# Eight unread products behind the first transposes of the maxima in both self attentions of a two-lane decoder, and the order of the two lanes written anew

## Chip, cores and metric

The kernel runs on one core of a Trainium2 chip, as one program. The metric is the device time of one execution in microseconds, the median of several runs. TensorE (PE) does the matrix products and the transposes, VectorE (DVE), ScalarE (ACT) and GpSimd (POOL) do the rest, and SyncE (SP) issues the DMAs. A profile comes from one more execution.

## What is computed

A pre-norm decoder of two layers runs over x of shape (4, 256, 128), with a context of the same shape. Each layer is a self attention, a cross attention and a feed-forward part, and each is added to x:

```python
x = x + _L0_attn_ref(_layernorm(x), Wq, Wk, Wv, rel_bias_table, ln_gamma, ln_beta)
x = x + _L0_xattn_ref(_layernorm(x), ctx, ctx, Wq, Wk, Wv, Wo, bo, mask)
x = x + _L0_ffn_ref(_layernorm(x), w1, conv_w, conv_b, w2)       # quantized, with a convolution
x = x + _L1_attn_ref(_layernorm(x), Wq, Wk, Wv, Wp, bp)          # causal, alibi, grouped keys
x = x + _L1_xattn_ref(_layernorm(x), ctx, ctx, ...)
x = x + _L1_ffn_ref(_layernorm(x), ...)                          # eight experts and a shared one
# the softmax of the first self attention, 16 heads of width 8:
attn = softmax(einsum('bhqd,bhkd->bhqk', q, k) * scale)
attn = attn + rel_bias_table[i - j + 255]
```

## The kernel before

The four batches are split over two lanes, A (batches 0 and 1) and B (batches 2 and 3). A lane is a full copy of the six stages with its own SBUF half and its own four PSUM banks, `bank[0]` to `bank[3]`; in the rows the names begin with `A_` or `B_`, and `l0a` and `l1a` are the two self attentions, `l0x` and `l1x` the cross attentions, `ffn` and `moe` the feed-forward parts. A third short program W (`weight_levels`) quantizes weights at the start, and L loads late weights.

Every engine works through one queue in program order. How the lanes share it is written out by hand in the table `TURNS`: for each engine a string such as `A4 W1 A7`, by which `merged` lets lane A emit four pieces, W one piece, A seven, and so on. A piece is what a lane's program emits between two `yield`s. So whatever stands first in an engine's queue and waits holds up what is behind it, the other lane's work too.

Both self attentions use the class `Attention`. It computes the scores twice:

- with queries on the partitions (`tensor_S` L226 and `tensor_S_pair` L296 in layer 0, L231 and L234 in layer 1), from which VectorE takes each row's maximum, negated (`vector_max`, L324), into `nmax`;
- with keys on the partitions (`tensor_E_pair` L310, or `tensor_E` L262, L263 and L266), whose exponentials ScalarE takes (`scalar_exp`, L358) for the products with the values (`tensor_PV`, L286).

For the second pass the maxima must stand in extra rows of the queries. `vector_parts` splits the maxima of a batch into three bf16 parts (L339 to L348), `tensor_shift` transposes them on TensorE into `bank[0]` (L242), `vector_shiftT` copies them to SBUF (L352), and `sync_shift` writes them into the queries by DMA (L252). The first `tensor_E` of a batch waits for that DMA. This is done once per lane, layer and batch of the lane (b = 0 and b = 1). For b = 1 the maxima are made during the second pass of b = 0.

Other rows that the text names: L662 transposes the stacks of split queries and keys, L647 projects x, L706 transposes finished outputs; L1247 and L1254 are the transposes and the last product of the quantized feed-forward part; L1616 transposes outputs in layer 1; L1816 is a product of a bf16 tile `same_token` with `other_token` (128x512) in the last cross attention. `bank[2]` is one of the two banks that the second pass writes into; between the transposes and the first E nothing in it is needed.

Of the kernel before, what the change touches and what calls it, by code (L numbers as in the profile page):

```python
# [175 lines left out]
class Attention:  # L176
# [59 lines left out]
        ins.then_inc(self.s_s.sem, 1)  # L236

    def tensor_shift(self, pe, b):
        pe.wait_ge(*self.s_parts(b + 1))
        view = self.bank[0][:, 0:P].bitcast(BF16)  # L240
        for c in range(SB):
            ins = pe.transpose(view[:, c * P:(c + 1) * P], self.parts[:, b, c, :], self.w["ident_bf"][:])  # L242
        ins.then_inc(self.s_tp.sem, 1)

    def sync_shift(self, sp, b):

        sp.wait_ge(*self.s_shT(b + 1))
        rows = P // self.G
        for j in range(self.G):
            dst = self.queries(b)[rows * j + self.row:rows * j + self.row + 3]  # L250
            src = self.shiftT[32 * j:32 * j + 3 * self.columns, b, :]
            sp.dma_start(dst, src).then_inc(self.s_q.sem, 16)  # L252
# [2117 lines left out]
def course(lane, name, eng):  # L2370

    for st in lane.plan:
# [9 lines left out]

TURNS = {
    "tensor":
# [8 lines left out]
    "vector":  # L2393
# [9 lines left out]
    "scalar":  # L2403
# [5 lines left out]
    "gpsimd":  # L2409
        "A12 B1 A3 B2 A1 B13 A11 B1 A1 B1 A1 B2 A1 B1 A2 B1 A1 B1 A1 B1 A2 B1 A1 B2 A2 B1 A1 B6 A1 B2 A1 B1 A3 B2 A1 B1 A1 B7 A8 B2 A2 B2 A1 B2 A2 B2 A1 B3 A1 "  # L2410
        "B1 A1 B2 A7 B1 A4 B3 A1 B1 A1 B9 A1 B1 A1 B2",
    "sync":
        "W3 A1 W10 B1 A2 B2 L1 A6 L1 A3 B5 A1 B5 A2 B2 A1 B1",
}


# [153 lines left out]
```

## Time and profile before

| | |
|---|---|
| time, median of 3 runs | 623.69 us (620.76 to 624.16) |
| the profiled execution, its own time | 619.47 us |
| its span, first to last instruction | 617.5 us |
| mean granted TensorE clock | 0.954 |
| busy share | PE 86%, PE weight loads 53%, DVE 69%, ACT 52%, POOL 31% |

The clock is given as a share of full speed: 1.0 is 2.4 GHz, 0.5 is 1.2 GHz. In a timeline row the numbers are the start and the length in us of a run of equal instructions, and the bracket at the end says how long the engine was idle before it and what ended that.

### The profile page before, as it was taken

The page shows a single profiled execution, that of the slowest core. Times are in us where ns is not written, and L with a number is a line of the kernel's source. Part 1 is how long each engine was busy: PE and PEld are TensorE (multiplying, and loading weights), DVE is VectorE, ACT ScalarE, POOL GpSimd, SP SyncE. Part 2 cuts the span into 40 slices and gives each one's busy share as a digit, 9 for nine tenths or more (in the row PEclk, how much of TensorE's full clock was granted, in tenths as well). Part 3 has the DMA queues.
Part 4 walks back from the last instruction along what each step waited for, and adds up shares of the span by engine and source line. Part 5 has one row for each costly group of instructions (what it writes and reads, how often), then busy time and mean ns, then how long its engine had stood idle before and what let it go on. Part 6 is the DMA issues. An engine that isn't in the chain of part 4 may idle for free. (4 is left out here: it accounts for less than half of the span.)

```text
span 617.5 us, 12861 instructions
## 1 busy us (share of the span) xinstructions
PE 529.0 (86%) x4880; PEld 327.9 (53%) x4890; DVE 424.6 (69%) x1037; ACT 323.5 (52%) x807; POOL 192.1 (31%) x288
## 2 busy tenths in 40 slices
PE   2668787999999999778986489978988999999894
PEld 1433343344555656446554355766666867655453
DVE  6885764654463654798779876847557577889994
ACT  1423445567576674695733536554666555362440
POOL 3743200043245443432620031001113122435653
PEclk9965999999999999989997889999999999999998
DMA  8700000000030000000256005300000000303001
GB/s 299 267 1 2 2 2 3 1 3 2 1 136 3 1 1 1 2 2 1 80 143 243 3 17 156 97 11 3 4 2 2 3 3 1 138 2 137 2 1 34
DMA packets 25815, 27.92 MB, mean 45 GB/s; under 512 B 18177, under 2 KB 22794, under 8 KB 24858
## 3 DMA queue, kind: packets, MB, share of 16 engines
q1 hardware_dynamic: 25754, 27.10, 13.1%
q8 instruction: 39, 0.64, 0.4%
q14 instruction: 22, 0.18, 0.1%
HBM read 22.14 MB, written 4.75 MB: 44 GB/s over the span
## 5 line engine op out<-in xcount | busy, mean ns | idle before, releaser
L811 POOL TENSOR_TENSOR A_l0x_prob<-A_l0x_prob,A_l0x_inverted_sums 128x256 f32<-128x256 f32 (+1 forms) x32 | 25.9, 829 | 56.6 <-DVE A_l0x_inverted_sums L922 56.6
L811 POOL TENSOR_TENSOR B_l0x_prob<-B_l0x_prob,B_l0x_inverted_sums 128x256 f32<-128x256 f32 (+1 forms) x32 | 26.5, 848 | 45.1 <-DVE B_l0x_inverted_sums L922 45.1
L2080 PE MATMUL B_banks<-B_moe_xT,w_moe_rows 128*128 128x512 f32 x72 | 33.8, 596 | 1.7 <-DVE B_moe_h L2047 1.7
L2080 PE MATMUL A_banks<-A_moe_xT,w_moe_rows 128*128 128x512 f32 x72 | 34.3, 597 | 0.0
L324 DVE TENSOR_REDUCE B_l0a_nmax<-B_banks 128x2 f32<-128x512 f32 x32 | 21.4, 688 | 15.2 <-PE B_banks L226 11.9
L905 DVE TENSOR_REDUCE A_l0x_nmax<-A_banks 128x2 f32<-128x256 f32 (+1 forms) x32 | 16.3, 552 | 22.6 <-PE A_banks L980 22.5
L358 ACT ACTIVATE A_l0a_expT<-A_banks 128x512 f32<-128x512 f32 x32 | 18.3, 599 | 22.0 <-PE A_banks L310 22.0
L829 ACT ACTIVATE B_l0x_prob<-B_banks,B_l0x_nmax 128x128 f32<-128x128 f32 x64 | 26.0, 420 | 5.9 <-DVE B_l0x_nmax L905 5.7
L324 DVE TENSOR_REDUCE A_l0a_nmax<-A_banks 128x2 f32<-128x512 f32 x32 | 21.3, 688 | 9.8 <-PE A_banks L226 8.0
L829 ACT ACTIVATE A_l0x_prob<-A_banks,A_l0x_nmax 128x128 f32<-128x128 f32 x64 | 26.1, 425 | 1.7 <-DVE A_l0x_nmax L905 1.7
L846 ACT ACTIVATE A_l0x_probT<-A_banks 128x384 f32<-128x384 f32 x32 | 15.8, 493 | 19.3 <-PE A_banks L992 19.1
L846 ACT ACTIVATE B_l0x_probT<-B_banks 128x384 f32<-128x384 f32 x32 | 15.7, 490 | 15.9 <-PE B_banks L992 15.8
L324 DVE TENSOR_REDUCE B_l1a_nmax<-B_banks 128x2 f32<-128x512 f32 (+1 forms) x24 | 16.2, 689 | 9.9 <-PE B_banks L234 9.7
L358 ACT ACTIVATE B_l0a_expT<-B_banks 128x512 f32<-128x512 f32 x32 | 18.6, 601 | 8.2 <-PE B_banks L310 8.1
L358 ACT ACTIVATE A_l1a_expT<-A_banks 128x384 f32<-128x384 f32 x32 | 15.3, 494 | 14.5 <-PE A_banks L266 14.5
L358 ACT ACTIVATE B_l1a_expT<-B_banks 128x384 f32<-128x384 f32 x32 | 15.5, 491 | 14.0 <-PE B_banks L266 13.9
L1976 ACT ACTIVATE B_moe_h<-B_banks,w_moe_rest_rows 128x512 f32<-128x512 f32 x18 | 12.3, 686 | 19.7 <-PE B_banks L2080 19.6
L2080 PEld LDWEIGHTS B_banks<-B_moe_xT,w_moe_rows 128*128 128x128 f32 x72 | 12.8, 190 | 14.7 <-issue 12.0
L905 DVE TENSOR_REDUCE B_l0x_nmax<-B_banks 128x2 f32<-128x256 f32 (+1 forms) x32 | 16.2, 548 | 5.9 <-PE B_banks L980 5.9
L1709 POOL TENSOR_TENSOR A_l1x_prob<-A_l1x_prob,A_l1x_rz 128x512 f32<-128x512 f32 x8 | 8.3, 1042 | 38.2 <-DVE A_l1x_rz L1790 38.2
L1976 ACT ACTIVATE A_moe_h<-A_banks,w_moe_rest_rows 128x512 f32<-128x512 f32 x18 | 12.1, 680 | 13.8 <-PE A_banks L2080 13.7
L992 PE MATMUL B_banks<-w_const_rows,B_l0x_prob 128*128 128x128 f32 x96 | 16.6, 283 | 3.0 <-POOL B_l0x_prob L811 1.4
(609 smaller groups left out, 1570.7 us busy)
## 6 DMA issues: line engine op xcount, KB each, us to landing
w_toeplitz_rows<-in_toeplitz_rows SPq DMA_DIRECT2D x1, 3072.0 KB, 15.3
w_moe_rows<-in_moe_rows SPq DMA_DIRECT2D x1, 2304.0 KB, 9.6
w_l1x_rows<-in_l1x_rows SPq DMA_DIRECT2D x1, 2048.0 KB, 7.8
A_l1x_values<-A_l1a_v_tokens SPq DMA_DIRECT2D x4, 512.0 KB, 3.5
A_l1x_v_groups<-A_l1x_values SPq DMA_DIRECT2D x16, 128.0 KB, 3.1
B_l1x_values<-B_l1a_v_tokens SPq DMA_DIRECT2D x4, 512.0 KB, 3.5
B_l1x_v_groups<-B_l1x_values SPq DMA_DIRECT2D x16, 128.0 KB, 3.1
w_l0x_vo_rows<-in_l0x_vo_rows SPq DMA_DIRECT2D x1, 1024.0 KB, 9.0
```

The lines of the kernel that those rows point to most:

```text
L324: dve.tensor_reduce(out, scores, AX, ALU.max, negate=True).then_inc(self.s_mx.sem, 1)
L358: act.activation(self.expT[:, u % self.ring, :], self.exp_bank(u)[:, 0:self.W], ACT.Exp, scale=self.scale).then_inc(self.s_p.sem, 1)
L811: ins = pool.tensor_tensor(pair, pair, bcast(rz[:, g % 2, i, :], 2, n), ALU.mult)
L829: ins = act.activation(prob[:, u % RING, at:at + n], bank[u % 2][:, at:at + n], ACT.Exp, bias=nmax[:, b, i, h:h + 1], accum_out=zsum[:, g ...
L846: act.activation(probT[:, u % 4, :], bank[2][:, 0:W], ACT.Copy).then_inc(s_pt.sem, 1)
L905: ins = dve.tensor_reduce(nmax[:, b, i, 2 * c:2 * c + 2], lane.banks[:, 0:2, at:at + n], AX, ALU.max, negate=True)
L992: ins = pe.transpose(bank[2][:, c * P:(c + 1) * P], prob[:, u % RING, c * P:(c + 1) * P], w["ident"][:])
L1709: pool.tensor_tensor(pr, pr, bcast(rz[:, n % 2, :], BL, 64), ALU.mult).then_inc(s_pn.sem, 1)
L1976: act.activation(h1[:, n % 2, :], hidden_bank(2 * n)[:, :], ACT.Identity, bias=w["moe_b1"][:, e, part:part + 1]).then_inc(s_h1.sem, 1)
L2080: pe.matmul(hidden_bank(k)[:, :], w["moe_w3" if which else "moe_w1"][:, ORDER[i], part, :], xT[:], start=True, stop=True).then_inc(s_h.sem, 1)
```

## The change

Two things are edited. In `tensor_shift`, for b = 0 alone, eight matrix products of the bf16 identity with the 128x512 tile `other_token` follow the two transposes. They write `bank[2]`, each with `start=True`, and nobody reads it. They wait for nothing of their own and signal nothing. That is four times in the program: lanes A and B, layers 0 and 1, so 32 products. And all five strings of `TURNS` are written anew.

```diff
     def tensor_shift(self, pe, b):
         pe.wait_ge(*self.s_parts(b + 1))
         view = self.bank[0][:, 0:P].bitcast(BF16)
         for c in range(SB):
             ins = pe.transpose(view[:, c * P:(c + 1) * P], self.parts[:, b, c, :], self.w["ident_bf"][:])
         ins.then_inc(self.s_tp.sem, 1)
+        if b == 0:
+            for _ in range(8):
+                pe.matmul(self.bank[2][:, :], self.w["ident_bf"][:], self.w["other_token"][:].rearrange("p i k -> p (i k)"), start=True,
+                          stop=True, skip_group_check=True)
...
 TURNS = {
     "tensor":
-        "A4 W1 A7 W1 A20 B1 A4 B1 A1 B1 A3 B1 A3 B1 A3 B1 A1 B1 A1 B1 A3 B1 A2 B2 A3 B1 A2 B2 A5 B2 A2 B1 A3 B1 A2 B2 A5 B3 A2 B3 A3 B1 A3 B1 A1 B4 A4 B1 A2 B2 "
+        "A4 W1 A6 W1 A23 B2 A2 B1 A2 B1 A6 B1 A4 B1 A2 B2 A2 B1 A5 B2 A2 B1 A3 B1 A1 B1 A1 B1 A3 B1 A1 B1 A1 B3 A6 B3 A2 B3 A2 B3 A4 B3 A2 B1 A1 B1 A1 B1 A2 B1 "
...
     "sync":
-        "W3 A1 W10 B1 A2 B2 L1 A6 L1 A3 B5 A1 B5 A2 B2 A1 B1",
+        "W2 A1 W11 B1 A2 B2 L1 A6 L1 A3 B5 A1 B5 A2 B2 A1 B1",
```

In the changed kernel all lines behind the new ones are six higher: L310 is L316, L286 is L292, L1247 is L1253. The order of TensorE's instructions at lane A's first maxima, layer 0, before:

```order
L172 MATMUL B_banks<-w_const_rows,B_l0a_xn 128x128 x4
L296 MATMUL A_banks<-A_l0a_qkT 128x256 x4
L647 MATMUL B_banks<-w_l0a_rows,B_l0a_xT 128x384
L662 MATMUL A_banks<-w_ident_bf,A_l0a_expT 128x128 x4
L242 MATMUL A_banks<-w_ident_bf,A_l0a_parts 128x128 x2
L647 MATMUL B_banks<-w_l0a_rows,B_l0a_xT 128x384
L310 MATMUL A_banks<-A_l0a_qkT 128x256 x4
L226 MATMUL A_banks<-A_l0a_qkT 128x256 x2
```

The same place in the changed kernel:

```order
L653 MATMUL B_banks<-w_l0a_rows,B_l0a_xT 128x384
L302 MATMUL A_banks<-A_l0a_qkT 128x256 x4
L653 MATMUL B_banks<-w_l0a_rows,B_l0a_xT 128x384
L668 MATMUL A_banks<-w_ident_bf,A_l0a_expT 128x128 x4
L244 MATMUL A_banks<-w_ident_bf,A_l0a_parts 128x128 x2
L248 MATMUL A_banks<-w_other_token,w_ident_bf 128x512 x8
L316 MATMUL A_banks<-A_l0a_qkT 128x256 x4
L226 MATMUL A_banks<-A_l0a_qkT 128x256 x4
```

B's second projection, which stood between the transposes and the first E, now stands before the transposes, and the eight products are what is left between them.

TensorE at lane A's first maxima in layer 1, while lane B is at the end of its quantized feed-forward part, before:

```order
L242 MATMUL A_banks<-w_ident_bf,A_l1a_parts 128x128 x2
L1247 MATMUL B_banks<-w_ident_bf,B_ffn_q_228 128x128 x4
L262 MATMUL A_banks<-A_l1a_qT,A_l1a_kT 128x256
L263 MATMUL A_banks<-A_l1a_qT,A_l1a_kT 128x128
L266 MATMUL A_banks<-w_mask_k,w_ident_bf 128x128 x2
L231 MATMUL A_banks<-A_l1a_kT,A_l1a_qT 128x256 x2
```

And in the changed kernel:

```order
L244 MATMUL A_banks<-w_ident_bf,A_l1a_parts 128x128 x2
L248 MATMUL A_banks<-w_other_token,w_ident_bf 128x512 x8
L1253 MATMUL B_banks<-w_ident_bf,B_ffn_q_228 128x128 x16
L1260 MATMUL B_banks<-w_ffn_q,B_ffn_q2T 128x128 x16
L268 MATMUL A_banks<-A_l1a_qT,A_l1a_kT 128x256
L269 MATMUL A_banks<-A_l1a_qT,A_l1a_kT 128x128
```

The first E of lane A now stands behind all 16 transposes and all 16 products of lane B's feed-forward part; before, four transposes stood ahead of it.

TensorE at lane B's first maxima in layer 0, in the changed kernel; before, the same rows stood there without L248:

```order
L316 MATMUL A_banks<-A_l0a_qkT 128x256 x4
L244 MATMUL B_banks<-w_ident_bf,B_l0a_parts 128x128 x2
L248 MATMUL B_banks<-w_other_token,w_ident_bf 128x512 x8
L712 MATMUL A_banks<-w_const_rows,A_l0a_xT 128x128 x2
L316 MATMUL A_banks<-A_l0a_qkT 128x256 x4
```

Here work of lane A follows the products at once.

## Rows read from the trace of the kernel before

**Rows 1.** The page: span, TensorE's busy share and its granted clock in 40 slices.

```profile
span 617.5 us, 12861 instructions
...
PE   2668787999999999778986489978988999999894
...
PEclk9965999999999999989997889999999999999998
```

**Rows 2.** Busy time by window (columns PE, PEld, DVE, ACT, POOL, then the clock).

```profile
42.00:48.80 6.80, 2.77 (x22) 1.32 (x21) 3.61 (x11) 3.13 (x9) 4.09 (x11) 1.00 0.01 4
48.80:62.50 13.70, 12.73 (x81) 5.28 (x80) 7.16 (x14) 4.16 (x11) 2.68 (x8) 0.50 0.00 1
...
349.20:356.00 6.80, 3.70 (x28) 3.07 (x29) 3.73 (x9) 3.80 (x6) 0.00 (x0) 0.50 0.02 6
...
120.00:240.00 120.00, 118.00 (x895) 64.61 (x888) 62.54 (x181) 80.56 (x265) 47.33 (x63) 1.00 0.05 19
```

**Rows 3.** Timeline at lane A's first maxima, layer 0.

```profile
43.43 0.27 PE L242 MATMUL A_banks<-w_ident_bf,A_l0a_parts 128*128 128x128 bf16 x2 [0.73 <-ACT A_l0a_qkT L511]
...
43.54 0.86 PE L647 MATMUL B_banks<-w_l0a_rows,B_l0a_xT 128*128 128x384 f32 x2
43.74 0.29 DVE L352 COPY A_l0a_shiftT<-A_banks 128x256 bf16<-128x256 bf16 x1 [0.16 <-PE A_banks L242]
...
44.06 1.66 SPq L252 DMA_DIRECT2D A_l0a_qkT<-A_l0a_shiftT  x2
...
47.24 0.39 PE L310 MATMUL A_banks<-A_l0a_qkT 64*128 64x256 bf16 x4 [2.83 <-DMA A_l0a_qkT<-A_l0a_shiftT]
```

**Rows 4.** TensorE's timeline at the low clock and, from 68 us, at the full one.

```profile
49.90 0.60 PE L226 MATMUL A_banks<-A_l0a_qkT 64*128 64x256 bf16 x2 [0.36 <-DVE A_l0a_nmax L324]
...
57.80 0.61 PE L226 MATMUL A_banks<-A_l0a_qkT 64*128 64x256 bf16 x2
58.34 1.93 PE L286 MATMUL A_banks<-A_l0a_expT,A_l0a_vals 128*32 128x256 f32 x16
...
61.91 0.61 PE L310 MATMUL A_banks<-A_l0a_qkT 64*128 64x256 bf16 x4
...
68.38 1.07 PE L286 MATMUL A_banks<-A_l0a_expT,A_l0a_vals 128*32 128x256 f32 x16
...
70.25 0.39 PE L310 MATMUL A_banks<-A_l0a_qkT 64*128 64x256 bf16 x4
...
71.65 0.39 PE L226 MATMUL A_banks<-A_l0a_qkT 64*128 64x256 bf16 x2 [0.57 <-DVE A_l0a_nmax L324]
...
72.84 0.39 PE L226 MATMUL A_banks<-A_l0a_qkT 64*128 64x256 bf16 x2 [0.48 <-DVE A_l0a_nmax L324]
```

**Rows 5.** A product of the same shape elsewhere: duration ns min/median/max.

```profile
L1816 PE MATMUL A_banks<-w_other_token,w_same_token x4: 379/379/379, 437.0 to 466.5; 128*128 128x512 bf16 x4
```

**Rows 6.** TensorE's timeline at lane B's first maxima, layer 0.

```profile
93.99 0.29 PE L242 MATMUL B_banks<-w_ident_bf,B_l0a_parts 128*128 128x128 bf16 x2
95.01 0.44 PE L706 MATMUL A_banks<-w_const_rows,A_l0a_xT 128*128 128x128 f32 x2 [0.74 <-ACT A_l0a_xT L549]
```

**Rows 7.** The same at lane B's first maxima, layer 1.

```profile
404.14 0.29 PE L242 MATMUL B_banks<-w_ident_bf,B_l1a_parts 128*128 128x128 bf16 x2
404.26 0.27 PE L262 MATMUL A_banks<-A_l1a_qT,A_l1a_kT 128*128 128x256 bf16 x1
...
405.56 0.44 PE L1616 MATMUL A_banks<-w_const_rows,A_l1a_v_tokens 128*128 128x128 f32 x2 [0.58 <-ACT A_l1a_v_tokens L1428]
```

**Rows 8.** The same at lane A's first maxima, layer 1.

```profile
348.09 0.28 PE L242 MATMUL A_banks<-w_ident_bf,A_l1a_parts 128*128 128x128 bf16 x2 [2.92 <-DVE A_l1a_parts L348]
351.29 0.61 PE L1247 MATMUL B_banks<-w_ident_bf,B_ffn_q 128*128 128x128 bf16 x4 [2.92 <-ACT B_ffn_r L1128]
352.91 0.40 PE L262 MATMUL A_banks<-A_l1a_qT,A_l1a_kT 128*128 128x256 bf16 x1 [1.01 <-DMA A_l1a_qT<-A_l1a_shiftT]
...
357.60 1.07 PE L1254 MATMUL B_banks<-w_ffn_q,B_ffn_q2T 128*128 128x128 bf16 x16
```

More of the change, by code:

```diff
@@ L2384 @@
     "tensor":
[8 rows of a table removed]
-    "vector":
[9 rows of a table removed]
-    "scalar":
[5 rows of a table removed]
[8 rows of a table added]
+    "vector":
[9 rows of a table added]
+    "scalar":
[5 rows of a table added]
     "gpsimd":
-        "A12 B1 A3 B2 A1 B13 A11 B1 A1 B1 A1 B2 A1 B1 A2 B1 A1 B1 A1 B1 A2 B1 A1 B2 A2 B1 A1 B6 A1 B2 A1 B1 A3 B2 A1 B1 A1 B7 A8 B2 A2 B2 A1 B2 A2 B2 A1 B3 A1 "
-        "B1 A1 B2 A7 B1 A4 B3 A1 B1 A1 B9 A1 B1 A1 B2",
+        "A12 B1 A3 B2 A1 B13 A11 B1 A1 B3 A2 B1 A2 B1 A1 B1 A1 B1 A2 B1 A1 B2 A2 B1 A1 B6 A1 B2 A1 B1 A2 B1 A1 B1 A1 B1 A1 B7 A8 B2 A2 B2 A1 B2 A2 B2 A1 B3 A1 "
+        "B1 A1 B2 A7 B1 A3 B2 A1 B2 A1 B2 A1 B7 A1 B1 A1 B2",
     "sync":
-        "W3 A1 W10 B1 A2 B2 L1 A6 L1 A3 B5 A1 B5 A2 B2 A1 B1",
+        "W2 A1 W11 B1 A2 B2 L1 A6 L1 A3 B5 A1 B5 A2 B2 A1 B1",
 }
```

42 rows, old and new, of the table TURNS are left out of this document.

## The prediction

> **What bounds the kernel now.** I read the page's slices first. TensorE is the busiest engine with 86% of the span; its share is 0.9 or more from the eighth slice to the sixteenth and again towards the end, and lower in the first seven and, deepest, in slices 22 and 23 [rows 1]. The windows say the same with numbers: from 120 to 240 us it is busy for 118.00 of 120.00 us, while DVE and ACT are busy for 62.54 and 80.56 [rows 2]. There every matrix product that is added costs its full time. In the other stretches no single engine is full, and what counts is the chain from engine to engine in queues that work in order.
>
> Second, the clock. The slices show it below 0.9 mainly in the third and fourth and again near 330 to 360 us [rows 1]. A mean of 0.954 over 617.5 us with only the levels 0.5 and 1.0 means 0.046 / 0.5 x 617.5, about 57 us, at 1.2 GHz. The first of these stretches that touches the change is 48.80 to 62.50 us: clock 0.50, and TensorE busy for 12.73 of 13.70 us [rows 2]. Just before it, from 42.00 to 48.80, the clock was full, but TensorE was busy for 2.77 of 6.80 us only [rows 2]. The timeline shows why it was idle: the transposes of A's maxima start at 43.43, the copy follows at 43.74, the DMA is issued at 44.06, and the first E starts at 47.24 after 2.83 us of idle time that the DMA ended [rows 3]. So the eight products of lane A, layer 0, fall into a hole, and behind this hole the engine works at half speed for 13.7 us.
>
> **What one product costs.** The changed operation has a sister in the trace: a bf16 product of 128x512 takes 379 ns from start to end at the full clock [rows 5]. Products in a row overlap: 16 of 128 columns take 1.07 us [rows 8], and one such takes about 0.22 us, so each further one costs (1.07 - 0.22) / 15 = 0.057 us per 128 columns, 0.227 us per 512. (The 0.22 is my reading of a pair that ends after 0.28 [rows 8], less one step of 0.057.) Eight are then 8 x 0.227 = 1.8 us at the full clock and, at half the clock, 3.6 us. The bounds are 1.8 and 8 x 0.379 = 3.0 at full clock; I take 1.8, since the 16 in a row are the same kind of run. The four places hold 32 products, 7.3 us of TensorE time in all.
>
> **Lane A, layer 0.** After the transposes TensorE has from 43.70 (43.43 + 0.27) to 47.24, 3.54 us, until the DMA lands [rows 3]. B's projection of 0.86 us that stood there now stands ahead, so 1.8 us of products lie wholly in the hole: cost nothing. If the DMA landed at once, they would cost 1.8. What they may bring is the full clock behind the hole. Two terms. First the rounds of scores and maxima: from the L226 at 49.90 to the one at 57.80 are five rounds, 7.90 us; a round at the full clock, 71.65 to 72.84, is 1.19 us, so five are 5.95 at best and 1.95 is the most that they give back [rows 4]. The least is five times the shorter L226, 0.60 - 0.39 = 0.21, so 1.05. I take 1.6, nearer the upper end, because other matrix work stands between the rounds and shrinks as well. Second the products with the values: from 58.34 to the next E at 61.91 is 3.57 us, from 68.38 to 70.25 is 1.87 us, for the same 32 products [rows 4]: 1.7. Together -3.3 us. Lower bound of the gain: 0, if the clock falls anyway. Upper bound: half of 12.73 us, -6.4 [rows 2].
>
> **Lane A, layer 1.** The transposes end at 348.37, and the next TensorE work, B's L1247, starts at 351.29 after 2.92 us of idle time [rows 8]. TensorE had also been idle for 2.92 us before the transposes, and from 349.20 the clock is 0.50 [rows 2]. I expect the products to run mostly at half clock here, so 3.6 us, to about 352.0: L1247 is late by about 0.7 us if it stays where it was. In return the clock may be back before 356.00. TensorE is busy for 3.70 us in that stretch [rows 2], so at most half of that, 1.85, comes back; I take 1.2. Net -0.5 us, with bounds -1.85 and +0.7.
>
> **Lane B, both layers.** Here other work follows at once. In layer 0 the next instruction starts at 95.01 after 0.74 us of idle time [rows 6]; 1.8 - 0.74 is +1.1 us on lane A's chain from the transposed outputs to the next group of values. In layer 1, L262 follows directly, and 0.58 us of idle time stands before L1616 at 405.56 [rows 7]: +1.2 us. The clock is full at both places, so there is nothing to win. Bounds for each: 0, if waits further on swallow it, and 1.8.
>
> **The new order.** Counted at every fortieth of lane A's matrix instructions, lane B stands within 16 instructions of where it stood, so the rewrite is local. At lane A's start in layer 0 one projection of B (0.86 us [rows 3]) moves ahead of the last scores and one ahead of the transposes, and it is the same work on the same engine: 0, with bounds -0.9 and +0.9. SyncE issues A's context two loads earlier, ahead of which other starting work still waits; I count nothing. At lane A's first E in layer 1, 12 more transposes and 16 products of lane B stand ahead. For the forecast I take 0, because B then ends its feed-forward part earlier by what A starts later, and the price if A's chain decides is the rival below. For all the places that I can't price, some 3 us either way is my allowance, half the spread of the terms above.
>
> **Sum.** -3.3 - 0.5 + 1.1 + 1.2 = -1.5 us. The profiled execution took 619.47 us, 1.97 more than its span, so it would take 618.0. The median of the runs, 623.69, is 4.2 above the profiled time, and I carry that over: 622.2 us.
>
> **A rule against it.** The low clock behind the hole costs 3.3 us here by the rows above, and all of the 57 us at 1.2 GHz can't be read as harmless when TensorE is 93% busy in 13.7 us of them [rows 2]. The Trainium skill, TensorE: Matmul & The Clock Gate, Part 1, says that the warm-up penalty is under 1% of a typical kernel's span and advises not to model it closely; the clock term would then be left out. This is the rival that follows.
>
> **Rival: the clock falls all the same.** The hole is 3.54 us and the products fill 1.8 of it; 1.7 us of idle time stay, while the idle time that stood before the fall was 2.83 in one piece and 0.73 ahead of the transposes [rows 3]. If the chip still lowers the clock, lane A gives nothing in layer 0 and costs up to 0.7 in layer 1, and lane B costs its 2.3: about +2.8 to +3.0, 626.6 us.
>
> **Rival: more comes back.** TensorE's work after 47.24 shrinks by the middle of my value and the upper bound, 4.9, layer 1 gives 1.2 and lane B costs half of its 2.3: -5.0, 618.7 us. For it speaks that the runs (620.76 to 624.16) lie above the profiled 619.47, so that some of them may have had the clock low for longer than this trace. Against it: ScalarE and VectorE stand in the same chain and don't get faster.
>
> **Rival, slower: lane A's first E in layer 1 waits behind lane B.** Before, it started at 352.91, and B's last product L1254 ended at 358.67 [rows 8]. In the new order it comes behind that. If B's part doesn't end sooner, E starts 5.8 us later; if it ends sooner by half, as the missing interleaving allows, 2.9. It decides as soon as E is later than B's gain, that is, when the next stretch is bound by lane A's chain. With the clock falling too: +2.8 + 2.9 = +5.7, 629.4 us.
>
> **Chances.** Forecast 0.40, more comes back 0.25, the clock falls all the same 0.17, A waits behind B 0.18. A measurement of this kernel tells about 0.5%, 3.1 us, from no change. Faster by more: the second case and about a quarter of the first, 0.36. Slower by more: the last and a part of the third, 0.23. Within it: 0.41. The range takes in the second and third cases with their spread and stops short of the last: 616.5 to 628.0 us. The likeliest case alone is 619.2 to 625.2, with the 3 us of the order.
>
> **What the profile after would show.** Right: eight L248 in the hole at about 44 us and TensorE idle for 1.5 to 2 us before the first E; the clock at 1.0 from there to 62 us; a round of L226 of about 1.2 us and the 32 products with the values in 1.9 us; the mean clock near 0.97 instead of 0.954; at lane B's two places no idle time behind L248 and the next work 1 us later. Wrong: the clock at 0.5 within some 5 us of the first E; or a full clock and the same times, because VectorE or ScalarE ends each round; or a first E in layer 1 that starts more than 3 us after its DMA has landed. The forecast also fails if the rewritten order opens waits of several us somewhere that the rows of before can't show.

## The result, and the profile after

The changed kernel takes 620.81 us (median of 20 runs, 618.93 to 622.50), the kernel before 623.02 us in the same comparison. The ratio is 0.9973 with a 95% interval of 0.9960 to 0.9986: 1.7 us less, inside the 0.5% that was counted as no change. (The two medians lie 2.2 us apart; gains in this document go by the ratio.) Single executions that took far longer, such as one of 2722 us, are left out of the ratios but not of the medians, which they move by 0.2 us at most. The forecast was 622.2 us by a sum of -1.5 us. Size and sign were right; most of what the sum is made of was not, as the traces and runs below show. That the total came out so close is luck.

The profiled execution after took 619.62 us; that of before took 619.47. So these two traces hold no gain at all. It has to be looked for in the list of all executions. The page of the changed kernel, answering to [rows 1]:

```profile
span 617.7 us, 12935 instructions
...
PE   4577788999999999768996679998998999999994
...
PEclk9965999999999999998997799999999999999998
```

The third and fourth slices, with the clock at 0.6 and 0.5, read exactly as before. The windows around lane A's first maxima in layer 0, and the two that answer to the other rows of [rows 2] (columns PE, PEld, DVE, ACT, POOL, then the clock):

```profile
28.00:42.00 14.00, 10.08 (x52) 5.06 (x53) 9.97 (x20) 1.79 (x3) 6.11 (x7) 0.53 0.00 1
42.50:49.30 6.80, 3.47 (x27) 1.49 (x25) 3.07 (x10) 3.08 (x8) 4.49 (x12) 1.00 0.01 4
49.30:63.00 13.70, 11.88 (x74) 4.62 (x72) 6.26 (x12) 4.32 (x12) 2.28 (x6) 0.50 0.00 1
120.00:240.00 120.00, 118.22 (x892) 64.02 (x892) 63.55 (x181) 80.21 (x264) 47.18 (x63) 1.00 0.05 19
...
349.20:356.00 6.80, 4.03 (x24) 2.56 (x25) 5.88 (x21) 2.42 (x4) 0.00 (x0) 0.79 0.01 2
```

TensorE worked 3.47 us ahead of the fall instead of 2.77, and the clock fell all the same: 13.7 us at 0.50, as long as before. TensorE's timeline through the hole and behind it, answering to [rows 3] and [rows 4]:

```profile
43.44 0.27 PE L244 MATMUL A_banks<-w_ident_bf,A_l0a_parts 128*128 128x128 bf16 x2 [0.73 <-ACT A_l0a_qkT L517]
43.55 1.89 PE L248 MATMUL A_banks<-w_other_token,w_ident_bf 128*128 128x512 bf16 x8
47.25 0.39 PE L316 MATMUL A_banks<-A_l0a_qkT 64*128 64x256 bf16 x4 [1.81 <-DMA A_l0a_qkT<-A_l0a_shiftT]
...
58.04 0.60 PE L226 MATMUL A_banks<-A_l0a_qkT 64*128 64x256 bf16 x2 [0.79 <-DVE A_l0a_nmax L330]
58.58 1.93 PE L292 MATMUL A_banks<-A_l0a_expT,A_l0a_vals 128*32 128x256 f32 x16
...
62.15 0.61 PE L316 MATMUL A_banks<-A_l0a_qkT 64*128 64x256 bf16 x4
```

The eight products take 1.89 us, lie wholly in the hole and delay nothing: E starts at 47.25, before at 47.24. Behind them the products with the values need 58.58 to 62.15, the same 3.57 us as before. The costs were read rightly, the return was not.

Lane A's maxima in layer 1, answering to [rows 8], and lane B's in both layers, answering to [rows 6, 7]:

```profile
351.97 0.29 PE L244 MATMUL A_banks<-w_ident_bf,A_l1a_parts 128*128 128x128 bf16 x2 [3.97 <-DVE A_l1a_parts L354]
352.09 2.63 PE L248 MATMUL A_banks<-w_other_token,w_ident_bf 128*128 128x512 bf16 x8
354.51 1.91 PE L1253 MATMUL B_banks<-w_ident_bf,B_ffn_q 128*128 128x128 bf16 x16
357.55 1.07 PE L1260 MATMUL B_banks<-w_ffn_q,B_ffn_q2T 128*128 128x128 bf16 x16 [1.12 <-ACT B_ffn_q2T L1137]
358.45 0.27 PE L268 MATMUL A_banks<-A_l1a_qT,A_l1a_kT 128*128 128x256 bf16 x1
```

```profile
94.29 0.28 PE L244 MATMUL B_banks<-w_ident_bf,B_l0a_parts 128*128 128x128 bf16 x2
94.42 1.89 PE L248 MATMUL B_banks<-w_other_token,w_ident_bf 128*128 128x512 bf16 x8
96.14 0.38 PE L712 MATMUL A_banks<-w_const_rows,A_l0a_xT 128*128 128x128 f32 x2
...
406.58 0.28 PE L244 MATMUL B_banks<-w_ident_bf,B_l1a_parts 128*128 128x128 bf16 x2
406.69 1.89 PE L248 MATMUL B_banks<-w_other_token,w_ident_bf 128*128 128x512 bf16 x8
408.42 0.38 PE L1622 MATMUL A_banks<-w_const_rows,A_l1a_v_tokens 128*128 128x128 f32 x2
```

In layer 1 the clock was full when lane A's products began and fell while they ran: the stretch from 353.1 to 356.5 us is at 0.50, and the eight take 2.63 us, between the 1.8 and the 3.6 of the two levels. Lane A's first E starts at 358.45 instead of 352.91, straight behind lane B's last product and without idle time. Lane B's product itself did not move (357.55, before 357.60). The transposes alone are already 3.9 us later, so 1.7 us were added behind them. VectorE's copy of the transposed maxima, with the DMA issued after it, shows where:

```profile
348.41 0.29 DVE L352 COPY A_l1a_shiftT<-A_banks 128x256 bf16<-128x256 bf16 x1
...
353.20 0.28 DVE L358 COPY A_l1a_shiftT<-A_banks 128x256 bf16<-128x256 bf16 x1
```

The copy is 4.8 us later than before. Before, E started 4.5 us behind it when the DMA had landed; with the same 4.5 us the DMA lands at about 357.7 here, an estimate. So lane B's work held up the first E by some 0.7 us only. But the loss does not stay:

```profile
386.41 0.20 DVE L348 TENSOR_TENSOR A_l1a_parts<-A_l1a_rest,A_l1a_parts 128x32 bf16<-128x32 f32 x1
...
387.10 0.21 DVE L354 TENSOR_TENSOR A_l1a_parts<-A_l1a_rest,A_l1a_parts 128x32 bf16<-128x32 f32 x1
```

This is VectorE's last operation for the parts of lane A's second batch, first in the trace of before and then in that of the changed kernel. It starts at 387.10 instead of 386.41: of 5.5 us, 0.7 are left. At lane B in layer 0 the next work follows 1.85 us behind the transposes (96.14 - 94.29), before 1.02; so 0.8 us are added, where 1.1 were forecast. In layer 1 the same distance is 1.84 us (408.42 - 406.58), before 1.42 (405.56 - 404.14): 0.4 us added, where 1.2 were forecast.

### The profile page after: what moved, and what is told of

Read it like the earlier page. It is cut to its first block and busy times, and to the rows that moved or that the text cites. A ratio compares the mean times of both kernels' runs of the same rounds, so it can differ in the third digit from the quotient of the medians.

```text
span 617.7 us, 12935 instructions
## 1 busy us (share of the span) xinstructions
PE 539.3 (87%) x4922; PEld 331.1 (54%) x4922; DVE 415.4 (67%) x1037; ACT 322.5 (52%) x807; POOL 192.8 (31%) x288
## 5 line engine op out<-in xcount | busy, mean ns | idle before, releaser
L2086 PEld LDWEIGHTS B_banks<-B_moe_xT,w_moe_rows 128*128 128x128 f32 x72 | 12.8, 190 | 13.6 <-issue 11.7
L1982 ACT ACTIVATE B_moe_h<-B_banks,w_moe_rest_rows 128x512 f32<-128x512 f32 x18 | 12.3, 683 | 14.6 <-PE B_banks L2086 12.0
L330 DVE TENSOR_REDUCE A_l1a_nmax<-A_banks 128x2 f32<-128x512 f32 (+1 forms) x24 | 16.1, 685 | 4.6 <-PE A_banks L234 4.6
```

The lines of the kernel that those rows point to most:

```text
L330: dve.tensor_reduce(out, scores, AX, ALU.max, negate=True).then_inc(self.s_mx.sem, 1)
L1982: act.activation(h1[:, n % 2, :], hidden_bank(2 * n)[:, :], ACT.Identity, bias=w["moe_b1"][:, e, part:part + 1]).then_inc(s_h1.sem, 1)
L2086: pe.matmul(hidden_bank(k)[:, :], w["moe_w3" if which else "moe_w1"][:, ORDER[i], part, :], xT[:], start=True, stop=True).then_inc(s_h.sem, 1)
```

## The experiments

All ratios are to the kernel before, run on the same chip in the same call. In three calls its medians were 622.56, 622.65 and 622.38 us. "Low time" is (1 - mean clock) / 0.5 x span, the time at 1.2 GHz, of the median execution of a kernel. The executions of before themselves show what it is worth. The 35 of the first call took on average 624.07 us at a mean clock of 0.943 (8 of them), 622.86 at 0.948 (9), 621.84 at 0.951 (9), and 619.89 and 621.0 at 0.952 and 0.954 (4 each); one more, at 0.944, took 622.07. Over all 99 executions of before in the three calls a straight line gives 290 us per unit of clock, which is 0.23 us for each us at 1.2 GHz (290 x 0.5 / 620). That is how time and clock go together; whatever else differs between executions is in it. The profiled one, at 0.954, is from the upper end. The low time of a median execution moves in steps: before has 64.5 us in the first call and 60.8 in the two others, while the means of the three are 63.7, 63.5 and 62.7.

### First: products or order

All products with the old order. Against the changed kernel only `TURNS` is that of before.

> All 32 products with the order of before. Clock theory (the products keep TensorE's clock up behind the hole of lane A, layer 0, in a part of the executions): 1 to 2 us faster than before, as much as the changed kernel is, and mean clocks of its executions above those of before. Order theory (the 2 us come from the rewritten order, above all from lane A's context being loaded earlier, and the products only cost): 1 to 3 us slower than before, clocks as before. In the traced execution of the changed kernel the clock fell at 49.3 us although the products ran, which speaks for the order theory.

Measured: 624.22 us, 1.0027 (1.0005 to 1.0048), low time 59.8 us. **The products alone make the kernel 1.7 us slower**, though they have 4.7 us less low time than before (64.5).

The new order without products:

```diff
-        if b == 0:
-            for _ in range(8):
-                pe.matmul(self.bank[2][:, :], ...)
```

> The rewritten order without any product. Clock theory: not faster than before, 0 to 2 us slower, and with mean clocks below those of the changed kernel (0.949 to 0.959). Order theory: faster than the changed kernel, by up to the 2.3 us that lane B's products were priced at, so 3 to 4 us faster than before.

Measured: 625.61 us, 1.0052 (1.0027 to 1.0077), low time 76.8 us. **The new order alone costs 3.2 us.** Its 12.3 us more of low time, at 0.23 each, are 2.9 us: nearly all of it, if the line holds for this kernel too. The trace, of an execution with 72.0 us of low time against 56.8 in that of before, shows the longest piece:

```profile
42.00:49.00 7.00, 3.69 (x14) 1.28 (x12) 3.75 (x11) 1.55 (x5) 1.71 (x4) 0.50 0.01 2
49.00:62.00 13.00, 9.45 (x46) 3.83 (x46) 6.17 (x11) 5.36 (x14) 2.79 (x9) 0.50 0.00 1
30.30:64.50 34.20, 23.62 (x132) 10.76 (x132) 19.82 (x43) 8.98 (x22) 11.95 (x22) 0.50 0.01 1
```

```profile
26.21 0.40 PE L298 MATMUL A_banks<-A_l0a_qkT 64*128 64x256 bf16 x4 [0.20 <-ACT A_l0a_qkT L513]
...
46.05 0.37 PE L244 MATMUL A_banks<-w_ident_bf,A_l0a_parts 128*128 128x128 bf16 x2 [0.73 <-ACT A_l0a_qkT L513]
49.94 0.61 PE L312 MATMUL A_banks<-A_l0a_qkT 64*128 64x256 bf16 x4 [3.52 <-DMA A_l0a_qkT<-A_l0a_shiftT]
```

Before has two low pieces here, with 6.8 us of full clock between them [rows 2]. In this execution they are one piece of 34.2 us. The transposes come 2.6 us later than in the changed kernel (46.05 against 43.44), and the first E 2.7. But that is not the work of the clock: lane A's first scores already stand 2.5 us later, at 26.21 us, before the clock falls at 30.3. In the changed kernel they start at 23.71:

```profile
23.71 0.39 PE L302 MATMUL A_banks<-A_l0a_qkT 64*128 64x256 bf16 x4 [0.20 <-ACT A_l0a_qkT L517]
```

In the six traces with the old order these scores start between 25.89 and 26.17 us. Of the six with the new order two start them at 23.71 and 23.78 (the changed kernel and lane A alone), the four others between 25.88 and 26.47. So executions of the new order also differ in their first 24 us. What decides it, and how much of the +3.2 it is, no run here tells: an order with only its beginning rewritten was not run.

The old order with the first place alone, and with lane B's two places alone:

```diff
-        if b == 0:
+        if b == 0 and self.st.lane.name == "A" and self.st.name == "l0a":      # first place
+        if b == 0 and self.st.lane.name == "B":                                # lane B
```

> The order of before, eight products only behind lane A's first maxima in layer 0, where 2.8 us of idle time and one projection stood. Clock theory: 1.5 to 3.3 us faster than before, since nothing is paid at the other three places. Order theory, or the clock falls anyway: within 0.5 us of before. In the old order the eight products delay lane B's projection by 1.8 us, within the hole.

> The order of before, eight products at lane B's two places only, where other work follows at once and the clock is full. My sum: 2.3 us slower than before (1.1 in layer 0, 1.2 in layer 1). Rival: the delay is swallowed by waits further on, 0 to 0.5 us.

Measured: the first place 620.18 us, 0.9974 (0.9954 to 0.9994), low time 56.9 us. Lane B 624.53 us, 1.0033 (1.0014 to 1.0053), low time 61.0 us. **The first place gains 1.6 us, lane B's places cost 2.0 us.** With 7.6 us less low time than before in the median (5.6 in the mean), the clock line gives 1.3 to 1.8 us for the first place. Lane B pays although its low time is no longer than before's: it is the work. Of the lane B kernel, and of the next one, there is no trace to read. That of the first place alone shows the hole and what follows it:

```profile
40.90:51.20 10.30, 6.43 (x44) 3.05 (x42) 6.55 (x16) 5.49 (x16) 4.56 (x12) 1.00 0.01 2
51.20:61.40 10.20, 9.84 (x64) 4.24 (x62) 5.15 (x11) 2.05 (x5) 2.28 (x6) 0.50 0.01 2
```

The full stretch around the hole is 10.3 us long here instead of 6.8, and the low one behind it 10.2 instead of 13.7. In the old order all three traces with products in this place have 10.2 to 10.3 us behind the hole, and all three without have 13.6 to 13.7. Yet the low time from 47 to 90 us is not plainly less: 20.4 us here and 20.6 with all products, because further low pieces stand at 68 to 72 and 75 to 82 us; 17.1 in both traces of before, 23.8 with lane A's layer 1 alone, and 17.0 in the old-order run with 14 further products, told below. So these traces show that the pattern behind the hole changes, not what that saves.

### Second: what in the first place does it

Fifteen products instead of eight in the first place, old order (`range(15)`), so that little idle time is left in the hole:

> The order of before, 15 products instead of 8 at lane A's first place in layer 0 and none elsewhere. 15 take 3.4 us, so that with the projection behind them TensorE is busy until about 47.7 us, some 0.5 us after the DMA has landed. If the clock falls because of the idle time that eight products leave, the fall at about 50 us now goes away in all executions: time at 1.2 GHz about 12 us less than with eight (56.9), and 2 to 3 us faster than with eight, so 616.5 to 618.5. If the clock falls because of the stretch behind the hole, where the rounds of maxima leave TensorE idle too, it comes out as with eight or 0.5 us slower.

Measured: 622.50 us, 0.9997 (0.9976 to 1.0017), low time 57.1 us. Low time is that of the kernel with eight (56.9), where 12 us less were expected if idle time in the hole were the cause: nearly filling the hole gives no less low time. And it costs 1.4 us more, about the seven further products at 0.227 = 1.6. That the eight are worth having because they end before the DMA is a reading of these two times; no trace shows where the fifteen end.

The new order with the first place alone, and with both places of lane A:

> The rewritten order, eight products at lane A's place in layer 0 alone. The rewritten order without products was 625.6 with 76.8 us at 1.2 GHz, the changed kernel 620.8 with 57.0. Theory 1 (the first place does all of the gain, lane B's products cost 2 us in this order too): 618 to 619. Theory 2 (the rewritten order was made around lane B's products, and hides them): as the changed kernel, 620 to 621.5.

> The rewritten order, eight products at lane A's places in both layers, none in lane B. Against the kernel with the first place alone: my sum says 0.5 us faster for lane A's place in layer 1, with bounds -1.85 and +0.7; the rival says no difference, since the clock there is down before the products begin. Against the changed kernel: what lane B's 16 products cost in this order, 2 us or nothing.

Measured: first place 621.50 us, 1.0000 (0.9974 to 1.0026), low time 65.5 us; lane A 621.08 us, 0.9989 (0.9968 to 1.0010), low time 57.4 us. In the new order the first place gives 3.2 us (from 1.0052, with the two intervals 1.0 to 5.5) and 11.3 us less low time. Lane A's layer 1 gives about 0.7 us more, which these intervals don't separate from nothing. Adding lane B's places leads to the changed kernel, at 0.9973. **In the new order lane B's sixteen products cost nothing** that can be measured (-1.0 us, with the two intervals -2.5 to +0.5); in the old one they cost 2.0 us.

The changed kernel with the first place's products 16 columns wide: the same instructions in the same order, but hardly any work.

```diff
-                pe.matmul(self.bank[2][:, :], self.w["ident_bf"][:], ...
+                n = 16 if self.st.lane.name == "A" and self.st.name == "l0a" else 512
+                pe.matmul(self.bank[2][:, 0:n], self.w["ident_bf"][:], ...
```

> The changed kernel, but the eight products at lane A's place in layer 0 have 16 columns instead of 512: the same number of instructions in the same order, hardly any work. If it is the work that holds the clock: 65 to 77 us at 1.2 GHz instead of 57.0, and 3 to 5 us slower than the changed kernel, so 624 to 626. If it is a matter of the order of instructions alone: as the changed kernel, 620.8.

Measured: 622.89 us, 1.0002 (0.9986 to 1.0017), low time 65.8 us against 56.8 of the changed kernel. **The gain hangs on the work, not on the instructions**: 1.8 us come with the 512 columns, and with the two intervals 0.6 to 3.1. Low time came out as expected of the work; the time lies 1.1 us below the expected 624 to 626. Its trace:

```profile
42.00:49.00 7.00, 3.75 (x21) 1.66 (x20) 3.75 (x11) 1.69 (x5) 1.85 (x5) 0.50 0.01 2
...
29.80:67.30 37.50, 27.11 (x162) 12.63 (x162) 20.75 (x45) 10.17 (x25) 13.25 (x26) 0.50 0.01 2
```

```profile
45.91 0.37 PE L244 MATMUL A_banks<-w_ident_bf,A_l0a_parts 128*128 128x128 bf16 x2 [0.73 <-ACT A_l0a_qkT L518]
46.07 0.41 PE L249 MATMUL A_banks<-w_other_token,w_ident_bf 128*128 128x16 bf16 x8
49.81 0.61 PE L317 MATMUL A_banks<-A_l0a_qkT 64*128 64x256 bf16 x4 [3.33 <-DMA A_l0a_qkT<-A_l0a_shiftT]
```

Again one low piece, of 37.5 us. It is tempting to say that the full products prevent this piece, and the order of events speaks against it. In all seven traces with full products in this place the clock is back before they run: at 42.5 in the changed kernel (products from 43.55), at 42.1 with the first place alone in the new order (products at 45.64). That return cannot be their doing. Whether an execution comes to the hole with the clock still low is settled before it. What the products can act on is what happens from there. No trace shows a full product of this place running into a low clock, so how they shorten the low time is not seen, only that less of it goes with them: in the times and mean clocks of twelve or more executions of each kernel.

### Third: is more of the same worth more

The changed kernel with two more unread products behind each pair of score groups in lane A's first rounds, 14 in all, into a bank of lane B that is free once the program that quantizes weights is done, for which the first of them waits:

```diff
+        if self.st.lane.name == "A" and m >= 2:
+            if m == 2:
+                pe.wait_ge(*self.w["levels"])
+            for _ in range(2):
+                pe.matmul(self.st.lane.spare[3][:, :], self.w["ident_bf"][:], ...)      # 128x512
```

> The changed kernel, and in lane A's first pass of scores in layer 0 (about 27 to 42 us, clock 0.5 in every trace so far) two more 512-column products after each pair of heads from the second pair on, 14 in all, into a bank of lane B that nobody uses yet. If a lack of work lowers the clock there, and its return at 42 us or later depends on chance, the low stretch from 28 to 42 shrinks or goes, low time falls from 57 us to 45 or less, and the time by 1 to 3 us against the changed kernel (617.8 to 619.8), at most, because VectorE was busy for 11.9 of 13.7 us in those rounds. If the rounds belong to VectorE alone and the clock falls later all the same: 620.3 to 621.

And the same 14 with the first place alone in the old order:

> The same 14 products added to the order of before with eight products at lane A's place in layer 0 alone (620.2, 56.9 us at 1.2 GHz). Expected as there: 617.5 to 619.5 and low time under 45 us, or no difference.

Measured: 620.14 us, 0.9967 (0.9948 to 0.9985), low time 48.8 us; and 621.19 us, 0.9984 (0.9965 to 1.0003), low time 47.1 us. The clock did what was wanted:

```profile
28.00:42.00 14.00, 10.63 (x77) 5.45 (x78) 11.70 (x24) 2.80 (x7) 8.63 (x14) 0.88 0.01 3
49.50:63.10 13.60, 11.78 (x75) 4.68 (x73) 6.42 (x12) 4.11 (x11) 2.38 (x7) 0.50 0.00 1
```

0.88 in the first rounds where the changed kernel has 0.53. Low time stayed above the 45 us that were expected. Yet 8.0 us less low time bring 0.4 us, not the 1.9 of the clock line, and in the old order 9.8 us less bring none (0.9974 to 0.9984). The intervals are wide enough (-1.0 to +1.8 us around the 0.4) that the line's 1.9 is only just outside. For the rounds the trace shows why a fast TensorE brings little: VectorE is busy for 11.70 of 14.00 us, and TensorE waits for its maxima:

```profile
34.08 0.39 PE L302 MATMUL A_banks<-A_l0a_qkT 64*128 64x256 bf16 x4 [0.62 <-DVE A_l0a_nmax L336]
```

From one group of scores to the next the time is 1.77 us here at the full clock and 1.99 in the changed kernel at the low one. What follows the rounds gains more, so that from lane A's first scores to the transposes this trace takes 17.5 us (26.36 to 43.82) and the changed kernel 19.7 (23.71 to 43.44): 2.3 us less, with the clock at full for most of it. But this execution started the scores 2.65 us later, one of the late starts told above. The 14 products' own time, some 3 us by 0.227 each, is in the measured sum too. This version is the fastest median here, but its interval covers that of the changed kernel.

Lane A's layer 1 alone, old order, and the kernel before once more:

> The order of before, eight products at lane A's place in layer 1 alone. My sum priced this place at 0.5 us faster, with bounds -1.85 and +0.7. All four places cost 1.7 us in the old order, the first place alone gave 1.6 and lane B's two cost 2.0, which leaves +1.3 for this one if they add up. Adding-up theory: 1.3 us slower than before. My sum: 0.5 us faster.

> The kernel before, once more, for a second trace. Its executions have mean clocks from 0.943 (about 624 us) to 0.954 (about 620 us), and the trace on record is one of the latter. If the slower ones are those in which the clock doesn't come back at 42 us, a trace with a mean clock of 0.943 to 0.948 shows one low stretch from about 30 to 62 us or longer; a trace at 0.951 to 0.954 looks like the one on record.

Measured: 621.13 us, 0.9990 (0.9970 to 1.0010), low time 57.6 us against 60.8 of before in this call; the gain of 0.6 us is within the interval. Five of its twelve executions had a clock of 0.943 to 0.949, with the first place alone one of twelve was that low. The +1.3 of the adding-up theory lies outside the interval (-1.9 to +0.6 us). The kernel before took 619.57 us at a clock of 0.954, and its trace is that of the first one again (low from 48.9 to 62.6). There is no trace of an execution of before at 0.943.

Adding work in the later rounds too, in lane B's first bank, wasn't tried: VectorE reads that bank at the time.

## Why the prediction was right, and where it was not

**Right in the sum.** -1.5 us forecast, -1.7 measured. Of the 1.4 us between 622.2 and 620.81, 0.7 are the base: three runs gave 623.69 for the kernel before, twenty gave 623.02. The other 0.7 are the change: -1.5 in the sum, -2.2 between the medians. The terms behind the total were not right, and their errors cancelled.

**Right in the costs.** 0.227 us for each product in a row: eight took 1.89 us, which is 0.38 + 7 x 0.216. Nothing in the first hole: E moved by 0.01 us. Lane B +2.3 forecast, +2.0 measured with the order of before. (In the changed kernel's trace only 0.8 and 0.4 us are added there, and nothing in its time.) Lane A layer 1 -0.5 forecast, -0.6 and -0.7 measured, neither apart from zero.

**The step that failed: "what they may bring is the full clock behind the hole".** I took -3.3 us from five rounds and 32 products at the full clock between 48.8 and 62.5. In the trace that stretch is as slow as before, to the hundredth for the products with the values, and the sign of being wrong that I had named, the clock at 0.5 within some 5 us of the first E, came after 2.1 us (47.25 to 49.3). The rival "the clock falls all the same" describes the trace, and its price, +2.8 us, was wrong as well, because the first place does gain: 1.6 us in the old order, 1.8 within the changed kernel. The gain measured half of what was taken, and it came on another path than the one that I had: of the 99 executions of before 42 have a mean clock below 0.949, of the changed kernel none of 20. That the gain comes from fewer executions with a low mean clock fits these lists; it is not shown, and how the products do it stays open. I had the sign of this in hand (all three runs of before lay above the profiled 619.47) and used it only for a rival. (A slip beside it: 0.25 and a quarter of 0.40 make 0.35, not 0.36.)

**The term taken as zero: the new order.** It is +3.2 us alone and, with all products, -3.4 us (1.0027 to 0.9973). I had allowed 3 us either way for places that I couldn't price. What stands there is an interaction: in the new order lane B's products cost nothing instead of 2.0, and the low time it brings by itself goes with the first place's products. The low times of the two kernels with all products are near each other (59.8 and 56.8 us: 0.7 us by the line), so most of the 3.4 is not in the low time. How well the queues hide 7.3 us of work and the earlier start of lane A in some executions are both left as reasons; no run separates them.

**The rival "A's first E waits behind B"** came neither as it was told nor as a price. The first E is 5.5 us later, but 4.8 of these were there at VectorE's copy, ahead of lane B's products. Of the 5.5 us 0.7 are left after 29 us, and 0.4 at the last group of products (612.22, before 611.85). The lateness did not last, so the stretch was not bound by lane A's chain alone, the very point it was said to hang on.

**What stays open.** In the old order the parts add up to -1.6 + 2.0 - 0.6 = -0.2 us and together measure +1.7. The intervals of the four ratios together allow some 2.5 us, so these 1.9 us may be noise, and no single row holds them. In the traces the kernel with all products is 0.4 us behind the one with the first place alone up to 250 us, 1.9 around 300, and 1.4 at the end. And which part of the five rewritten strings costs or helps was never tried apart.

**The clock and the rule.** In the runs 12.3 us more at 1.2 GHz went with 3.2 us, and executions of one kernel differ by 4 us with their clocks. The Trainium skill, TensorE: Matmul & The Clock Gate, Part 1, calls the warm-up penalty under 1% of a typical kernel's span. The 3.2 us are 0.5%, but they are only a difference: by the line above, all 57 us at 1.2 GHz would be worth 13 us, 2.1% of the span, an estimate. The page's advice for modelling is not to fit a certain count of slow products. To leave the clock out altogether, as the prediction read it, would here have left out what most goes with either edit.

## What to carry to other kernels

Unread products are worth a trial where TensorE is idle for a transfer and they end before it lands, and not where other work follows at once: in the old order the same eight gained 1.6 us in one place and cost about 1 us each time in lane B. Before the clock of one trace goes into a sum, list the mean clock of many executions: here the profiled one was of the best kind. Before two traces are compared in the middle, see whether they began alike: 2.5 us of difference stood there before anything that the comparison was about. And measure filler and order apart as well as together: +1.7 and +3.2 us became -1.7.

## What was not expected of the hardware

- The clock fell at 49.3 us behind 1.81 us of idle time as it had behind 2.83, and 15 products instead of 8 gave no less low time (57.1 and 56.9 us).
- One kernel's executions differ in mean clock: before took about 624 us at 0.943 and 620 to 621 at 0.952 to 0.954. After the change none of 20 was below 0.949.
- 8 to 9 us less at 1.2 GHz went with 1.6 to 1.8 us at one place and with 0.4 at another, though the intervals overlap.
- With the old order lane A's first scores started within 0.3 us of each other in six traces; with the new one they lay 2.7 us apart (23.71 to 26.47).
